# A two-layer mixture-of-experts kernel: x put in x1's column order by GpSimd ahead of time, and one exponential moved between two copies on ScalarE

## The chip, the cores and the metric

The kernel runs on one NeuronCore of a Trainium2 chip. The metric is the device time in microseconds, lower is better. TensorE (PE) multiplies matrices out of SBUF into PSUM, VectorE (DVE) and ScalarE (ACT) work on SBUF and PSUM, GpSimd (POOL) works on SBUF, and SyncE (SP) does nothing here but start transfers. Each engine runs its own list of instructions in order; they meet through semaphores.

## What is computed

The input x has 128 samples of 32 channels by 512 columns. Two layers follow one another, each adding to x:

```python
def cond0(x, embedding, ...):            # attention over 8 kernels, from the sample's embedding
    att = softmax(gelu(gelu(embedding @ W0 + b0) @ W1 + b1) @ W2 + b2)
    agg_w = einsum('bk,koi->boi', att, weight[..., 0])
    return einsum('boi,bih->boh', agg_w, x) + (att @ bias_k)[:, :, None]
def ffn0(y, W_up, gate_w, expert_bias, lora_A, lora_B):     # 4 experts of rank 8, top 1
    one_hot = argmax_one_hot(y @ gate_w.T + expert_bias)
    z = einsum('nh,erh->ner', y, lora_A)
    return y @ W_up.T + einsum('neh,ne->nh', einsum('ner,ehr->neh', z, lora_B), one_hot)
def cond1(x, c, weight, c_weight, bias):                    # 9-tap convolution in 4 groups
    out = conv1d(x, weight, pad=4, groups=4)
    return out + (c @ c_weight.T)[:, :, None] + bias[None, :, None]
def ffn1(c, W_base, b_base, W_gate, A, B):                  # 8 experts of rank 16, top 2
    route_w = top2_softmax_weights(c @ W_gate.T)
    h = einsum('bnd,erd->bner', c, A) * route_w[..., None]
    return c @ W_base.T + b_base + einsum('bner,eor->bno', h, B)
x = x + ffn0(cond0(x, cond_128, ...), ...)                  # called x1 below
out = x + ffn1(cond1(x, cond_128, ...), ...)
```

## The kernel before, in words

The 4096 rows (sample and channel) are cut into 32 tiles of 128 rows, that is 4 samples each. Matrix products run on float32 values split in two: a rounded high part (`y_hi`, `xq_hi`, `c_hi`) that ScalarE copies, and a low part (`y_lo`, `xq_lo`, `c_lo`), the difference, that GpSimd or VectorE computes; a product is then high by high, high by low and low by high.

Every engine has one function `body(i, par)`, called for i from 0 to 33. `iterate` (L241) writes out the calls 0 to 3 and 28 to 33 and makes a loop on the chip of 4 to 27, two to a turn. In `body(i)` three tiles are in work: tile i in layer 0, tile i-1 in layer 1's convolution and product, tile i-2 in the end of layer 1. `once(t)` is true where tile t exists, `after(engine, semaphore, count)` is a wait that is left out for counts of zero. `par` is i modulo 2: `xt`, the tile of x, has two buffers.

For tile t the work goes so. `mix` (L914) multiplies `xt` by the sample's weights; VectorE adds the bias into `y32`; `y_hi` on ScalarE and `y_lo` on GpSimd (L430) follow. TensorE then runs `up_half` for columns 256 to 511 with the gate (L854, L859, j = 1), and later for columns 0 to 255; `lora_delta` (L901) adds the expert's part. `x1_sum` (L674) adds x to that, in two halves, and writes `x1s`: x1 in another order of columns, p = (m j r) read as j, r, m, and shifted by one between the halves. SyncE and ScalarE copy `x1s` to `xq` with eight transfers of 32.5 KB (`move_x`, L277), five on SyncE's queue and three on ScalarE's; behind its five SyncE starts the load of tile t+2 into the same `xt` buffer (`load_x`, L284), then the store of an output. From `xq` come `xq_hi` (L507) and `xq_lo` (L415), each in two parts of 16 channels (gp = 0 and 1); GpSimd then computes `x1b` = x1 plus a bias in x's own order (L422), and `prod` (L369) for a tile further on.

TensorE's `body(i)` is, in order: `up_half` j = 1 of tile i; `conv(i-1, 0)`, with the transposition `turn_hw` in it; `conv(i-1, 1)`; `up_half` j = 0 of tile i, with the transposition `turn_z` in it; `lora_delta(i)`; the experts' product of tile i-2 (L987); `mix(i+1)`; the base product of tile i-1 (L1004 and L1009), whose first half writes over a PSUM bank that VectorE's `out_sum` (L708) has to have read. Each `conv(t, gp)` has four products of `xq_hi` and then two of `xq_lo`, for which it waits.

VectorE's order around the two places: `turn_c` of part 0, `z_low`, `turn_c` of part 1, `x1_sum(i)`, `out_sum` j = 0 of tile i-2, the two halves of `c_lo`, `out_sum` j = 1, `y_sum(i+1)`. In the gate of layer 1 the largest two logits (`m81`, L723) go to ScalarE for an exponential (`e2`, L501), and come back to VectorE for the route and `hw` (L740), which TensorE transposes in `turn_hw`. On ScalarE the exponential stands first in `body(i)`, then the two parts of `xq_hi`.

Of the kernel before, what the change touches and what calls it, by code (L numbers as in the profile page):

```python
# [5 lines left out]
ALU = mybir.AluOpType  # L6
# [6 lines left out]
P = 128  # L13
B = 128
C = 32
H = 512
SPT = P // C
NT = B // SPT
NQ = 4
# [12 lines left out]
GP = 2  # L32
# [12 lines left out]
def adaln_ffn(nc, x, cond, fside, W0, b0, W1, b1, W2, b2, wmix, bias_k, w_up, gate_w,  # L45
# [6 lines left out]
    with ExitStack() as ctx:  # L52
# [6 lines left out]
        def bank(name, banks=1):  # L59
# [57 lines left out]
        prod, gsum = sb("prod", [P, C, KATT]), sb("gsum", [P, C])  # L117
        mix_w = sb("mix_w", [P, SPT, C])
        y32, y_hi, y_lo = sb("y32", [P, KC, P]), sb("y_hi", [P, KC, P], F32R), sb("y_lo", [P, KC, P], F32R)
        gl0, m80, ix0 = sb("gl0", [P, 8]), sb("m80", [P, 8]), sb("ix0", [P, 8], U32)  # L120
# [45 lines left out]
                                                           sem("zt_done"), sem("zT_ready"))  # L166
        upgate_done, basegate_done = sem("upgate_done"), sem("basegate_done")
        lb_done, x1_done, x1b_done = sem("lb_done"), sem("x1_done"), sem("x1b_done")
        xqhi_done, xqlo_done, ct_done = sem("xqhi_done"), sem("xqlo_done"), sem("ct_done")
# [179 lines left out]
        def _(pool):  # L349
# [21 lines left out]


            pool.wait_ge(in_small0, 64)
            for n in range(3):
# [29 lines left out]
            pool.wait_ge(in_gate, 16)  # L404
            order_rows(g1_p, g1_raw, g1p_ready)
            pool.wait_ge(in_b1, 16)
            pool.tensor_copy(b1m_t[:], b1m_raw[:].rearrange("m e q r -> m q e r")).then_inc(b1_copied, 1)

            def body(i, par):
                if once(i - 1):  # L410

                    for gp in range(GP):
                        pool.wait_ge(xqhi_done, 2 * i - 1 + gp)
                        pool.wait_ge(xq_in[gp], i * XQ)
                        pool.tensor_tensor(xq_lo[:, gp], xq[:, gp], xq_hi[:, gp], ALU.subtract)\  # L415
                            .then_inc(xqlo_done, 1)
                    if isinstance(i, int) and i == 1:
                        pool.wait_ge(in_rows, 32)
                    pool.wait_ge(x1_done, 2 * i)
                    after(pool, out_done, (i - 2) * 2)  # L420
                    for j in range(2):
                        pool.tensor_tensor(columns_of(x1b[:, 1 - par])[:, j], shifted(j), columns_of(bbase_s[:])[:, j],  # L422
                                           ALU.add).then_inc(x1b_done, 1)
                if once(i + 3):
                    make_prod(i + 3)
                if once(i + 1):

# [7 lines left out]
        def _(act):  # L435
# [16 lines left out]
            def high_part(n):  # L452
# [6 lines left out]
                else:  # L459
                    act.activation(fills[n][4], fill_bank(n), ACT.Copy).then_inc(fill_hi, 1)  # L460

            def z_high(t):
# [33 lines left out]

            def body(i, par):
                if once(i - 2):

                    act.wait_ge(m81_ready, i - 1)  # L500
                    act.activation(e2[:], m81[:, 0:1], ACT.Exp, bias=m81[:, 1:2], scale=-1.0).then_inc(e2_ready, 1)  # L501
                if once(i - 1):

                    for gp in range(GP):
                        act.wait_ge(xq_in[gp], i * XQ)
                        after(act, conv_done, 2 * i - 3 + gp)
                        act.activation(xq_hi[:, gp], xq[:, gp], ACT.Copy).then_inc(xqhi_done, 1)  # L507
                if once(i - 2):
# [33 lines left out]
        def _(dve):  # L542
# [122 lines left out]
            def x1_sum(t, par):  # L665
# [4 lines left out]
                after(dve, xq_in[1], t * XQ)  # L670
                after(dve, x1b_done, 2 * t)
                for j in range(2):
                    dve.wait_ge(lb_done, 2 * t + j + 1)
                    dve.tensor_tensor(shifted(j), ps_up[:, j, 0:HALF].rearrange("p (r m) -> p r m", r=NQ),  # L674
                                      columns_of(xt[:, par])[:, j], ALU.add).then_inc(x1_done, 1)

# [361 lines left out]
```

## Time and profile before

| | |
|---|---|
| median of 3 runs | 380.35 us (377.62 to 380.48) |
| the profiled execution, its own time | 379.92 us |
| its span | 378.1 us, so 1.8 us lie outside the span |
| TensorE busy | 356.5 us, 94% of the span |
| VectorE, GpSimd, ScalarE busy | 284.5, 179.4, 135.5 us |

The span runs from the first to the last instruction. A matmul's end is modelled, and matmuls overlap, so that TensorE's pace is read from the distances between their ends. Times in the views are microseconds from the span's start; a name's digits are left out there (`y32` is y, `c32` is c, `e2` is e).

### The profile page before, as it was taken

To read this page: it belongs to the slowest core of one execution; us is meant where nothing else is said; L and a number is where in the kernel's file an instruction comes from. 1 tells how busy PE (TensorE), PEld (TensorE's weight loads), DVE (VectorE), ACT (ScalarE), POOL (GpSimd) and SP (SyncE) were. 2 spreads that over 40 slices of the span, in tenths; PEclk is the share of its full clock that TensorE was granted. 3 is DMA by queue.
4 is the path that set the end of the run, shared out by engine and by line. 5 is a ranking of instruction groups with operands and counts; after the bars stand their busy time and mean duration, and the time that the engine had idled before them with its cause. 6 is when DMAs were issued, how large, how long until landed. Compare 5 with 4: busy or idle time off the path is not lost.

```text
span 378.1 us, 8986 instructions
## 1 busy us (share of the span) xinstructions
PE 356.5 (94%) x2589; PEld 343.6 (91%) x2589; DVE 284.5 (75%) x966; ACT 135.5 (36%) x409; POOL 179.4 (47%) x223
## 2 busy tenths in 40 slices
PE   2877999999999999999999999999999999999975
PEld 1666999999999999999999999999999999999964
DVE  1675768787887887777788788777877878877653
ACT  2634243333333434433333343443333333343321
POOL 5364455544445455554444545555444454444430
PEclk9998699999999999999999999999999999999999
DMA  7622245343323323333332333333333233234221
GB/s 163 187 85 30 93 123 149 86 85 76 62 59 78 76 72 81 84 84 84 84 59 59 74 77 73 77 84 84 84 84 78 42 74 78 72 77 86 56 58 56
DMA packets 49983, 30.92 MB, mean 82 GB/s; under 512 B 39684, under 2 KB 40116, under 8 KB 49968
## 3 DMA queue, kind: packets, MB, share of 16 engines
q1 hardware_dynamic: 35744, 26.60, 28.2%
q10 hardware_dynamic: 13984, 3.73, 6.6%
q0 software_dynamic: 240, 0.41, 0.4%
q8 instruction: 7, 0.11, 0.1%
q14 instruction: 8, 0.07, 0.1%
HBM read 13.79 MB, written 8.40 MB: 59 GB/s over the span
## 4 chain that ended last, share of the span: by engine, by line
PE 86%; DVE 2%; POOL 1%; ACT 1%; DMA 1%; issue 1%; ACTq 1%; DVEq 0%; POOLq 0%
PE ps_base L1004 21%; PE ps_up L854 17%; PE ps_base L1009 10%; PE ps_up L859 8%; PE ps_mix L914 7%; PE ps_conv L876 6%; PE ps_mix L876 6%; PE ps_base L987 6%; PE ps_up L901 2%; PE ps_turn L893 1%; DMA xq<-x1s 1%; PE ps_turn L885 1%; ACTq L277 1%; POOL base_p L388 1%; PE ps_base L814 1%
## 5 line engine op out<-in xcount | busy, mean ns | idle before, releaser
L430 POOL TENSOR_TENSOR y_lo<-y,y_hi 128x512 fp32r<-128x512 f32 x31 | 40.1, 1295 | 141.0 <-ACT y_hi L478 141.0
L1004 PE MATMUL ps_base<-base_hi,c_hi 128*128 128x392 f32 (+1 forms) x256 | 78.6, 323 | 2.5 <-ACT c_hi L526 1.3
L1004 PE MATMUL ps_base<-base_lo,c_hi 128*128 128x392 f32 (+1 forms) x256 | 75.2, 311 | 0.0
L854 PE MATMUL ps_up<-up_hi,y_hi 128*128 128x292 f32 (+1 forms) x256 | 72.2, 304 | 1.2 <-ACT y_hi L478 1.2
L854 PE MATMUL ps_up<-up_lo,y_hi 128*128 128x292 f32 (+1 forms) x256 | 69.5, 293 | 0.0
L581 DVE TENSOR_TENSOR mix_w<-gsum,quad 128x64 f32<-128x64 f32 x64 | 39.2, 616 | 33.2 <-PE ps_base L1009 32.1
L415 POOL TENSOR_TENSOR xq_lo<-xq,xq_hi 128x260 fp32r<-128x260 f32 x64 | 46.6, 745 | 34.5 <-ACT xq_hi L507 24.8
L422 POOL TENSOR_TENSOR x1b<-x1s,bbase_s 128x256 f32<-128x256 f32 x64 | 57.0, 923 | 0.0
L1004 PEld LDWEIGHTS ps_base<-base_hi,c_hi 128*128 128x128 f32 x256 | 48.2, 188 | 8.2 <-issue 4.8
L854 PEld LDWEIGHTS ps_up<-up_hi,y_hi 128*128 128x128 f32 x256 | 49.2, 192 | 1.4 <-ACT y_hi L478 1.3
L478 ACT ACTIVATE y_hi<-y 128x512 fp32r<-128x512 f32 x32 | 20.2, 632 | 82.2 <-DVE y L591 78.9
L854 PEld LDWEIGHTS ps_up<-up_lo,y_hi 128*128 128x128 f32 x256 | 49.2, 192 | 0.0
L1009 PE MATMUL ps_base<-base_hi,c_lo 128*128 128x392 f32 (+1 forms) x256 | 48.4, 311 | 0.0
L1004 PEld LDWEIGHTS ps_base<-base_lo,c_hi 128*128 128x128 f32 x256 | 48.2, 188 | 0.0
L859 PE MATMUL ps_up<-up_hi,y_lo 128*128 128x292 f32 (+1 forms) x256 | 43.7, 293 | 0.0
L1009 PEld LDWEIGHTS ps_base<-base_hi,c_lo 128*128 128x128 f32 x256 | 40.4, 188 | 0.0
L674 DVE TENSOR_TENSOR x1s<-ps_up,xt 128x256 f32<-128x256 f32 x64 | 38.0, 636 | 2.2 <-PE ps_up L901 1.0
L859 PEld LDWEIGHTS ps_up<-up_hi,y_lo 128*128 128x128 f32 x256 | 37.0, 191 | 0.4 <-POOL y_lo L430 0.4
L914 PE MATMUL ps_mix<-mix_w,xt 128*128 128x128 f32 x256 | 33.8, 275 | 0.1
L507 ACT ACTIVATE xq_hi<-xq 128x260 fp32r<-128x260 f32 x64 | 26.5, 415 | 15.7 <-DMA xq<-x1s 15.5
L473 ACT ACTIVATE c<-ps_conv,biasT 128x64 f32<-128x64 f32 x128 | 29.7, 315 | 6.3 <-PE ps_conv L876 3.1
L914 PEld LDWEIGHTS ps_mix<-mix_w,xt 128*128 128x128 f32 x256 | 31.3, 191 | 0.3 <-issue 0.3
(164 smaller groups left out, 639.5 us busy)
## 6 DMA issues: line engine op xcount, KB each, us to landing
xt<-in_x SPq DMA_DIRECT2D x32, 256.0 KB, 2.8
out_x<-ot SPq DMA_DIRECT2D x32, 256.0 KB, 2.8
xq<-x1s SPq DMA_DIRECT2D x160, 32.5 KB, 2.2
xq<-x1s ACTq DMA_DIRECT2D x96, 32.5 KB, 2.2
rows<-agg_rows SPq DMA_DIRECT2D x2, 597.0 KB, 3.9
wbase_raw<-in_L_ffn_W_base SPq DMA_DIRECT2D x2, 512.0 KB, 4.3
rows<-agg_rows SPq DMA_DIRECT2D x1, 598.0 KB, 4.0
wup_raw<-in_L_ffn_W_up ACTq DMA_DIRECT2D x2, 256.0 KB, 4.6
```

The costliest lines, as they stand in the source:

```text
L415: pool.tensor_tensor(xq_lo[:, gp], xq[:, gp], xq_hi[:, gp], ALU.subtract)\
L422: pool.tensor_tensor(columns_of(x1b[:, 1 - par])[:, j], shifted(j), columns_of(bbase_s[:])[:, j], ALU.add).then_inc(x1b_done, 1)
L430: pool.tensor_tensor(y_lo[:], y32[:], y_hi[:], ALU.subtract).then_inc(ylo_done, 1)
L473: act.activation(c32[:, 0, cols], ps_of[0][:, 0, cols], ACT.Identity, bias=biasT[:, 0, bass.ds(t * SPT + b, 1)]).then_inc(c32_done, 1)
L581: dve.tensor_tensor(mix_w[:, b2], gsum[:].unsqueeze(1).to_broadcast([P, SPT // 2, C]), quad[:, b2].unsqueeze(2).to_broadcast([P, SPT // 2, ...
L674: dve.tensor_tensor(shifted(j), ps_up[:, j, 0:HALF].rearrange("p (r m) -> p r m", r=NQ), columns_of(xt[:, par])[:, j], ALU.add).then_inc(x ...
L854: pe.matmul(into, y_hi[:, k], w[:, k, cols], start=(k == 0 and w is up_hi), stop=False, skip_group_check=True)
L859: mm = pe.matmul(into, y_lo[:, k], up_hi[:, k, cols], start=False, stop=(k == KC - 1), skip_group_check=True)
L876: mm = pe.matmul(ps_of[gp][:, 0, 0:HALF], w[:, gp, part], rhs[:, gp, :, part:part + NB], start=(n == 0 and part == 0), stop=(n == 2 and pa ...
L914: mm = pe.matmul(ps_mix[:, 0, k * P:(k + 1) * P], xt[:, par, k * P:(k + 1) * P], mix_w[:].rearrange("p b o -> p (b o)"), start=True, stop= ...
L1004: pe.matmul(ps_base[:, j, 0:width], c_hi[:, q], w[:, q, j, 0:width], start=(q == 0 and w is base_hi), stop=False, skip_group_check=True)
L1009: mm = pe.matmul(ps_base[:, j, 0:width], c_lo[:, q], base_hi[:, q, j, 0:width], start=False, stop=(q == NQ - 1), skip_group_check=True)
```

## The change

There is a new buffer `xtp` with two halves, one for each `xt` buffer. GpSimd's new `order_x(t, par)` copies tile t of `xt` into it in x1's column order, and `x1_sum` reads `xtp` where it read `xt` through `columns_of`; for that it waits on `xtp_done`. `order_x(0, 0)` stands in GpSimd's preparation. In GpSimd's `body(i)`, `order_x(i + 1, 1 - par)` stands behind `prod` and ahead of `y_lo`. The wait for the transfer that it reads (tile i+1 in `xt`, semaphore `x_in`) stands at the head of `body(i)`, ahead of both parts of `xq_lo`; only in `body(0)` it stands at the copy itself. On ScalarE the copy of `xq_hi` is now a function `x_high`, called for part 0 ahead of the exponential and for part 1 behind it.

```diff
--- before.py
+++ after.py
@@ -116,6 +116,7 @@
         xt = sb("xt", [P, 2, H])
         prod, gsum = sb("prod", [P, C, KATT]), sb("gsum", [P, C])
         mix_w = sb("mix_w", [P, SPT, C])
+        xtp = sb("xtp", [P, 2, H])
         y32, y_hi, y_lo = sb("y32", [P, KC, P]), sb("y_hi", [P, KC, P], F32R), sb("y_lo", [P, KC, P], F32R)
         gl0, m80, ix0 = sb("gl0", [P, 8]), sb("m80", [P, 8]), sb("ix0", [P, 8], U32)
         zm = sb("zm", [P, 3, Z0])
@@ -165,6 +166,7 @@
         up_done, gate0_step, z_ready, zt_done, zT_ready = (sem("up_done"), sem("gate0_step"), sem("z_ready"),
                                                            sem("zt_done"), sem("zT_ready"))
         upgate_done, basegate_done = sem("upgate_done"), sem("basegate_done")
+        xtp_done = sem("xtp_done")
         lb_done, x1_done, x1b_done = sem("lb_done"), sem("x1_done"), sem("x1b_done")
         xqhi_done, xqlo_done, ct_done = sem("xqhi_done"), sem("xqlo_done"), sem("ct_done")
         conv_done, c32_done, chi_done, clo_done = sem("conv_done"), sem("c32_done"), sem("chi_done"), sem("clo_done")
@@ -370,6 +372,11 @@
                                    ALU.mult).then_inc(prod_done, 1)
 
 
+            def order_x(t, par):
+
+                pool.tensor_copy(xtp[:, par].rearrange("p (j r m) -> p j r m", j=2, r=NQ), columns_of(xt[:, par]))\
+                    .then_inc(xtp_done, 1)
+
             pool.wait_ge(in_small0, 64)
             for n in range(3):
                 cp = pool.tensor_copy(lb_rep[:, :, n], lb_raw[:].rearrange("m e q r -> m q e r"))
@@ -403,12 +410,16 @@
             order_rows(a1_p, a1_raw, a1p_ready)
             pool.wait_ge(in_gate, 16)
             order_rows(g1_p, g1_raw, g1p_ready)
+            pool.wait_ge(x_in[0], 16)
+            order_x(0, 0)
             pool.wait_ge(in_b1, 16)
             pool.tensor_copy(b1m_t[:], b1m_raw[:].rearrange("m e q r -> m q e r")).then_inc(b1_copied, 1)
 
             def body(i, par):
                 if once(i - 1):
 
+                    if once(i + 1):
+                        pool.wait_ge(x_in[1 - par], (i + par) * 8 + 16)
                     for gp in range(GP):
                         pool.wait_ge(xqhi_done, 2 * i - 1 + gp)
                         pool.wait_ge(xq_in[gp], i * XQ)
@@ -424,6 +435,10 @@
                 if once(i + 3):
                     make_prod(i + 3)
                 if once(i + 1):
+                    if not once(i - 1):
+                        pool.wait_ge(x_in[1 - par], 16)
+                    order_x(i + 1, 1 - par)
+                if once(i + 1):
 
                     pool.wait_ge(y32_done, i + 2)
                     pool.wait_ge(yhi_done, i + 2)
@@ -459,6 +474,12 @@
                 else:
                     act.activation(fills[n][4], fill_bank(n), ACT.Copy).then_inc(fill_hi, 1)
 
+            def x_high(i, gp):
+
+                act.wait_ge(xq_in[gp], i * XQ)
+                after(act, conv_done, 2 * i - 3 + gp)
+                act.activation(xq_hi[:, gp], xq[:, gp], ACT.Copy).then_inc(xqhi_done, 1)
+
             def z_high(t):
 
                 act.wait_ge(zt_done, t + 1)
@@ -495,16 +516,14 @@
             act.activation(conv_columns(conv_hi), conv_turns(), ACT.Copy).then_inc(convhi_ready, 1)
 
             def body(i, par):
+                if once(i - 1):
+                    x_high(i, 0)
                 if once(i - 2):
 
                     act.wait_ge(m81_ready, i - 1)
                     act.activation(e2[:], m81[:, 0:1], ACT.Exp, bias=m81[:, 1:2], scale=-1.0).then_inc(e2_ready, 1)
                 if once(i - 1):
-
-                    for gp in range(GP):
-                        act.wait_ge(xq_in[gp], i * XQ)
-                        after(act, conv_done, 2 * i - 3 + gp)
-                        act.activation(xq_hi[:, gp], xq[:, gp], ACT.Copy).then_inc(xqhi_done, 1)
+                    x_high(i, 1)
                 if once(i - 2):
 
                     act.wait_ge(ht_done, i - 1)
@@ -669,10 +688,12 @@
                 after(dve, xq_in[0], t * XQ)
                 after(dve, xq_in[1], t * XQ)
                 after(dve, x1b_done, 2 * t)
+                dve.wait_ge(xtp_done, t + 1)
                 for j in range(2):
                     dve.wait_ge(lb_done, 2 * t + j + 1)
                     dve.tensor_tensor(shifted(j), ps_up[:, j, 0:HALF].rearrange("p (r m) -> p r m", r=NQ),
-                                      columns_of(xt[:, par])[:, j], ALU.add).then_inc(x1_done, 1)
+                                      xtp[:, par, j * HALF:(j + 1) * HALF].rearrange("p (r m) -> p r m", r=NQ),
+                                      ALU.add).then_inc(x1_done, 1)
 
             def z_low(t):
 
```

The loop on the chip, GpSimd, one turn's first half before; each row is an instruction with what it waits for (ISA and REGISTER_ALU rows are waits and address arithmetic):

```order
L414 REGISTER_ALU [waits xqhi_done]
L415 TENSOR_TENSOR xq_lo<-xq,xq_hi 128x260 [waits xq_in0]
L415 TENSOR_TENSOR xq_lo<-xq,xq_hi 128x260 [waits xq_in1,xqhi_done]
L235 ISA [waits x1_done]
L422 TENSOR_TENSOR x1b<-x1s,bbase_s 128x4x64 [waits out_done]
L422 TENSOR_TENSOR x1b<-x1s,bbase_s 128x4x64
L235 ISA
L369 ISA [waits gsum_done]
L369 TENSOR_TENSOR prod<-wmix_t,att_b 128x256
L428 REGISTER_ALU
L430 TENSOR_TENSOR y_lo<-y,y_hi 128x512 [waits yhi_done,y32_done]
```

The same place now, as far as the copy:

```order
L424 ISA [waits x_in1]
L425 REGISTER_ALU [waits xqhi_done]
L426 TENSOR_TENSOR xq_lo<-xq,xq_hi 128x260 [waits xq_in0]
L426 TENSOR_TENSOR xq_lo<-xq,xq_hi 128x260 [waits xq_in1,xqhi_done]
L237 ISA [waits x1_done]
L433 TENSOR_TENSOR x1b<-x1s,bbase_s 128x4x64 [waits out_done]
L433 TENSOR_TENSOR x1b<-x1s,bbase_s 128x4x64
L237 ISA
L371 ISA [waits gsum_done]
L371 TENSOR_TENSOR prod<-wmix_t,att_b 128x256
L377 COPY xtp<-xt 128x512
```

The wait for x's transfer (`x_in`) is the first thing in the turn, and a copy of 512 columns stands between `prod` and `y_lo`.

ScalarE, the same turn before, from the exponential on:

```order
L501 ACTIVATE e<-m 128x1 [waits m81_ready]
L505 REGISTER_ALU
L235 ISA [waits xq_in0]
L507 ACTIVATE xq_hi<-xq 128x260 [waits conv_done]
L235 REGISTER_ALU [waits xq_in1]
L507 ACTIVATE xq_hi<-xq 128x260 [waits conv_done]
L511 ACTIVATE hT_hi<-ps_turn 128x128 [waits ht_done]
```

and now:

```order
L237 ISA [waits xq_in0]
L481 ACTIVATE xq_hi<-xq 128x260 [waits conv_done]
L523 REGISTER_ALU
L524 ACTIVATE e<-m 128x1 [waits m81_ready]
L237 REGISTER_ALU [waits xq_in1]
L481 ACTIVATE xq_hi<-xq 128x260 [waits conv_done]
L530 ACTIVATE hT_hi<-ps_turn 128x128 [waits ht_done]
```

The exponential has moved behind part 0 of `xq_hi` and no longer stands ahead of it.

## Rows read from the trace of the kernel before

**Rows 1.** Busy time by stretch: stretch, length, engines busy, TensorE's granted clock, DMA share, GB/s.

```profile
38.00:44.00 6.00, 5.58 (x25) 5.25 (x25) 4.47 (x14) 1.81 (x7) 3.84 (x5) 0.50 0.36 146
200.00:320.00 120.00, 119.85 (x896) 117.17 (x895) 98.08 (x332) 43.17 (x138) 58.15 (x68) 1.00 0.34 73
364.00:378.00 14.00, 8.54 (x51) 7.06 (x50) 5.28 (x20) 3.16 (x11) 3.19 (x4) 1.00 0.18 61
```

**Rows 2.** Timeline, one body's tail: start, length, engine, instruction, count, idle before it.

```profile
201.81 1.21 DVE L674 TENSOR_TENSOR x1s<-ps_up,xt 128x256 f32<-128x256 f32 x2
202.40 1.05 PE L914 MATMUL ps_mix<-mix_w,xt 128*128 128x128 f32 x8
202.91 0.44 DVE L708 TENSOR_TENSOR ot<-ps_base,x1b 128x256 f32<-128x256 f32 x1
203.25 0.77 DVE L786 TENSOR_TENSOR c_lo<-ps_ct,c_hi 128x256 fp32r<-128x256 f32 x2
203.48 0.19 PEld L1004 LDWEIGHTS ps_base<-base_hi,c_hi 128*128 128x128 f32 x1 [0.22 <-issue]
```

**Rows 3.** Timeline of SyncE's queue, the same body.

```profile
203.05 3.45 SPq L277 DMA_DIRECT2D xq<-x1s  x5
206.72 0.41 SPq L284 DMA_DIRECT2D xt<-in_x  x1
```

**Rows 4.** The 24 loads of x issued from 85 to 335 us (L284).

```profile
L284 SPq DMA_DIRECT2D xt<-in_x x24: 341/376/590, 91.9 to 332.7; - x24
DMA to landing us min/median/max: 2.4/2.8/3.2
```

**Rows 5.** Timeline of GpSimd, the body that follows.

```profile
205.80 1.29 POOL L430 TENSOR_TENSOR y_lo<-y,y_hi 128x512 fp32r<-128x512 f32 x1 [4.39 <-ACT y_hi L478]
208.06 1.44 POOL L415 TENSOR_TENSOR xq_lo<-xq,xq_hi 128x260 fp32r<-128x260 f32 x2 [0.97 <-DMA xq<-x1s]
209.47 1.81 POOL L422 TENSOR_TENSOR x1b<-x1s,bbase_s 128x256 f32<-128x256 f32 x2
211.25 0.73 POOL L369 TENSOR_TENSOR prod<-wmix_t,att_b 128x256 f32<-128x256 f32 x1
```

**Rows 6.** Timeline of ScalarE and TensorE around the convolution, same body.

```profile
207.30 0.30 ACT L501 ACTIVATE e<-m 128x1 f32<-128x1 f32 x1 [1.64 <-DVE m L723]
207.50 0.41 ACT L507 ACTIVATE xq_hi<-xq 128x260 fp32r<-128x260 f32 x1
...
209.29 0.49 PE L876 MATMUL ps_conv<-xq_lo,conv_hi 128*128 128x256 f32 x2
...
212.29 1.18 DVE L674 TENSOR_TENSOR x1s<-ps_up,xt 128x256 f32<-128x256 f32 x2
```

**Rows 7.** Timeline near the end, where TensorE waits for `xq_lo`.

```profile
364.75 0.74 POOL L415 TENSOR_TENSOR xq_lo<-xq,xq_hi 128x260 fp32r<-128x260 f32 x1 [7.65 <-ACT xq_hi L507]
...
365.54 0.51 PE L876 MATMUL ps_conv<-xq_lo,conv_hi 128*128 128x256 f32 x2
```

**Rows 8.** Groups by shape: count, busy us, mean ns of one, idle before.

```profile
L674 DVE TENSOR_TENSOR x1s<-ps_up,xt 128x256 f32<-128x256 f32 x64 | 38.0, 636 | 2.2 <-PE ps_up L901 1.0
L708 DVE TENSOR_TENSOR ot<-ps_base,x1b 128x256 f32<-128x256 f32 x64 | 26.8, 420 | 0.7 <-PE ps_base L987 0.7
L565 DVE TENSOR_TENSOR base_lo<-ps_base,base_hi 128x512 fp32r<-128x512 f32 x3 | 2.1, 692 | 4.0 <-ACT base_hi L460 4.0
L565 DVE TENSOR_TENSOR b_lo<-ps_base,b_hi 128x512 fp32r<-128x512 f32 x1 | 1.1, 1112 | 0.3 <-ACT base_hi L460 0.3
L388 POOL COPY base_p<-wbase_raw 128x256 f32<-128x256 f32 x8 | 4.8, 642 | 0.0
```

**Rows 9.** Timeline, tiles 1 and 30, the ends of the stretch that repeats.

```profile
45.19 1.16 DVE L674 TENSOR_TENSOR x1s<-ps_up,xt 128x256 f32<-128x256 f32 x2 [0.41 <-PE ps_up L901]
...
348.23 1.19 DVE L674 TENSOR_TENSOR x1s<-ps_up,xt 128x256 f32<-128x256 f32 x2
```

## The prediction

> **What bounds the kernel now.** First the busy times by stretch: between 200 and 320 us TensorE is busy 119.85 of 120 us at a granted clock of 1.00, the full 2.4 GHz, while VectorE and GpSimd have 98.1 and 58.2 [rows 1]. So TensorE's list of work sets the pace, and only what holds TensorE up, or stops holding it up, moves the time. Then the two ends of the stretch that repeats: x1_sum of tile 1 starts at 45.19, of tile 30 at 348.23 [rows 9], so one body takes (348.23 - 45.19) / 29 = 10.45 us. Then the timeline of one body, for holes in TensorE's work. There is one: mix ends at 202.40 + 1.05 = 203.45, and the weight load of the base product starts at 203.48 after 0.22 us of idle time [rows 2]. The view gives "issue" as the reason, but that product also waits until out_sum j = 0 has read the bank, and out_sum runs from 202.91 to 203.35; it stands on VectorE behind the two x1_sums, which take 1.21 us. VectorE is thus on the path there, for about 0.22 us a body. Everywhere else the feeders come in time: xq_lo starts on GpSimd at 208.06, its first part is done at about 208.80, and TensorE takes it at 209.29 [rows 5, 6]. That slack is 0.5 us, and it matters below.
>
> **x1_sum reads xtp.** One x1_sum of 256 columns takes 636 ns, out_sum of 256 columns, PSUM and SBUF inputs too, 420 [rows 8]. The difference in form is that columns_of(xt) takes every eighth column. A second pair says that such a step costs: the low part b_lo, written and read in steps of four columns, took 1112 ns for 512, base_lo in long runs 692 [rows 8]. I take the new x1_sum at out_sum's price; a pair of such instructions takes 0.77 us (c_lo, [rows 2]), against 1.21, so 0.44 us less. The bounds are 0.77 and 1.21, the second if the step is not the cause. On the path this is worth at most the hole: out_sum would end before mix does, and 0.22 us a body is gained.
>
> The Trainium skill, "VectorE: DVE Perf Modes", section "Mode 1× (REGULAR) — the baseline", says that this mode makes no assumption on strides and gives one result per cycle, and its section "The TRN2 errata" gives (N + 151) / 0.96 ns for an fp32 tensor_tensor, 424 ns for 256 columns. By that rule the strided form should have cost 424 ns already and the excess would have another cause and stay; out_sum's row agrees with the figure, x1_sum's and b_lo's do not.
>
> **The copy order_x on GpSimd.** 512 columns in steps of eight: the nearest row is the COPY in steps of eight with 642 ns for 256 [rows 8], so 1.28 us a body; the bounds are that and 1.81, the time of the pair x1b with steps on two operands [rows 5]. It stands behind prod, which ends at 211.98, and ahead of y_lo, before which GpSimd is idle for 4.39 us in one body [rows 5]. That idle time is its cover, so it costs nothing; should GpSimd be late for y_lo by a microsecond, TensorE's y_lo products would wait for it. The copy for tile 0 stands in the preparation where GpSimd later idles too.
>
> **The exponential.** Before, ScalarE waits 1.64 us for the maximum from VectorE, does the exponential at 207.30, and part 0 of xq_hi at 207.50 [rows 6]. Now part 0 goes into that idle time. Its only reader before TensorE is xq_lo, which could start when y_lo ends, at 207.09, and not at 208.06 [rows 5]. TensorE needs neither before 209, so the gain is zero by itself; the worst is a body in which part 0 comes late and puts the exponential back by its 0.41 us, which the same slack of half a microsecond covers. I take zero.
>
> **The wait for x's transfer at the head of GpSimd's body.** This is the term that decides. In body i GpSimd now waits for tile i+1 in xt ahead of both parts of xq_lo. Who starts that transfer? SyncE, in its body i-1, behind the five copies of x1s of tile i-1, and xq_lo in GpSimd's body i works on just these copies. Before the change xq_lo depended on the copies; now it depends on the sixth transfer of the same queue as well. In the trace x1_sum ends at 203.02, the first copy starts at 203.05 and the load at 206.72 [rows 2, 3]; it lands 2.8 us after its issue, 2.4 to 3.2 over 24 loads [rows 4], here between 209.1 and 209.9 and by the median at 209.5. But xq_lo starts at 208.06 before the change [rows 5]. Behind the waiting GpSimd are queued both parts of xq_lo, x1b, prod and the copy; TensorE waits for xq_lo part 0 in conv(i-1, 0), and with it all that stands behind in its list, up to the x1_sum that starts the next load. So it is a closed loop that no slack can hide, and the new length of a body is its sum:
>
> - the pair of x1_sums, 0.77;
> - end of x1_sum to the start of the load, 206.72 - 203.02 = 3.70 [rows 2, 3];
> - the load's landing, 2.8 [rows 4];
> - GpSimd's start after it: xq_lo started 0.15 after xq_hi's end (207.50 + 0.41 to 208.06, [rows 5, 6]), and I take 0.2, as a wait and an address instruction now stand in between;
> - start of xq_lo part 0 to TensorE's first product on it, where TensorE does wait: 365.54 - 364.75 = 0.79 [rows 7];
> - that product to the next x1_sum: 212.29 - 209.29 = 3.00 [rows 6]. This piece is a chain through TensorE, ScalarE and VectorE, all behind the convolution, so it moves as a whole.
>
> The sum is 0.77 + 3.70 + 2.8 + 0.2 + 0.79 + 3.00 = 11.26 us, 0.81 more than 10.45. It holds 29 times between tiles 1 and 30: 23.5 us. (Tile 0 to 1 has room: TensorE runs there at half clock from 38 to 44 us [rows 1].) Behind tile 30 no load is left to wait for, and there the old gains come: 0.22 for the hole and 0.44 for the last x1_sum, 0.7 us. The profiled execution was 379.92, and 0.1% under the median of 380.35, so both serve: 379.92 + 23.5 - 0.7 = 402.7, **403 us**.
>
> The gain of the hole is not to be added: TensorE reaches the convolution earlier by it and waits there longer. The faster x1_sum is in the sum, since x1_sum itself is a part of the loop. x1b has to be ready for the next x1_sum: it ends 3.22 us after xq_lo's start [rows 5], x1_sum comes 0.79 + 3.00 = 3.79 after it, so 0.57 us are left.
>
> **The rivals.**
> First, the forecast's mechanism, with x1_sum unchanged at 636 ns: 0.44 more for 29 bodies and the last, 13 us, so 416. For it speaks the page's rule above, against it the two pairs of rows; chance 0.08.
>
> Second, the other side: the wait costs nothing, because x is there when GpSimd asks. It would have to land by about 208.3, the slack of 0.5 us behind xq_lo's present start used up; that is 1.6 us from the start of its issue, where the shortest of 24 took 2.4. Or the count that GpSimd waits for would be that of the tile before; but (i + par) * 8 + 16 is the count that mix waits for as tile i+1's. Then only the hole remains: 31 bodies by 0.22 and the last x1_sum, 7.3 us, so 373. The point where it flips is the landing at 1.6 us. Chance 0.06.
>
> Third, the same loop, but shorter: landing 2.4 and GpSimd's start 0.15, thus 10.81 a body, 13 us less, 390. A single load can be that quick, the mean of all hardly; chance 0.04.
>
> Fourth, TensorE's clock falls because of the new pauses of about a microsecond a body. It was at 0.50, that is 1.2 GHz, from 38 to 44 us after a start with holes, but at 1.00 in the last 14 us with TensorE busy 8.54 of 14 [rows 1], which is far emptier than the 10.2 of 11.3 to come. If the piece of 3.00 us ran at the low level in one body of four, it would add up to 3 us in each of those seven, 21 us: 424. Chance 0.03.
>
> **How the numbers follow.** The forecast as worked out has 0.79. Its own spread: landing 2.8 with a mean off by 0.15 gives 4 us either way, GpSimd's start between 0.15 and 0.3 gives -1.5 to +3, SyncE's 3.70 with 0.1 gives 3; so 396 to 411. To leave out no more than 2 in 10, the range goes up to the first rival: **395 to 417**. Left out are the second to fourth rivals. A change within 1% cannot be told from none for this kernel. Faster by over 1%: 0.06, the second rival. Within 1%: 0.02, for something between it and the forecast. Slower by over 1%: 0.92.
>
> **What would show it.** In the profile after: in GpSimd's timeline xq_lo part 0 starts right behind the landing of the load of x, not behind xq_hi, and the chain that ended last runs through the transfer xt<-in_x, GpSimd's xq_lo and VectorE's x1_sum, with a body of 11.3 us; TensorE is idle for about 1 us a body ahead of L876's products on xq_lo, and its busy share falls to about 90%; xq_hi part 0 ends a microsecond or more ahead of its xq_lo; the new COPY takes about 1.3 us with GpSimd idle behind it; x1_sum takes 0.42 us; and TensorE's clock stays at 1.00. The forecast is wrong if TensorE does not wait at that product, or if the load lands much sooner after its issue than it did.

## Result and the profile after

The changed kernel takes **407.23 us** (median of 4 runs, 405.49 to 408.67), the kernel before, run on the same chip, 380.17 (4 runs, 377.62 to 380.48). The ratio is 1.0726 with the interval 1.066 to 1.0791: slower by 7.3%. The forecast was 403, with a range of 395 to 417.

The profiled execution took 405.49, with a span of 403.7 us against 378.1 before. The page gives the same work for more time: TensorE has 355.6 us of it, 88% of the span. The shares of the engines in the chain of work that ended last read

```profile
PE 25%; SPq 18%; DMA 18%; issue 11%; POOL 8%; DVE 8%; ACTq 2%; ACT 2%; DVEq 1%; POOLq 1%
```

In the kernel before PE alone had 86% of that chain. Here SyncE's queue and the transfers hold 36% of it, and the lines named first behind this row are the copies of `x1s` (L279, 18%) and the load of x (`xt<-in_x`, 15%).

The busy times by stretch (stretch, length, busy time of TensorE, its weight loads, VectorE, ScalarE, GpSimd, granted clock, DMA share, GB/s) answer to [rows 1]:

```profile
38.00:44.00 6.00, 4.82 (x38) 4.43 (x37) 4.64 (x19) 2.10 (x8) 4.68 (x6) 1.00 0.34 133
44.00:56.00 12.00, 10.56 (x65) 10.06 (x64) 5.65 (x25) 3.68 (x12) 6.44 (x8) 0.86 0.38 98
200.00:320.00 120.00, 111.10 (x828) 108.62 (x828) 85.91 (x302) 41.60 (x128) 66.47 (x75) 1.00 0.30 67
```

TensorE is now idle for 8.9 of 120 us where it was idle for 0.15, and its clock is still at 1.00. The view of the waits (engine, operation, line and what it waited for: us in total, times, the longest) says for what:

```profile
POOL y_lo L445 <- ACT y_hi L499: 81.9, 31, 4.2
POOL xq_lo L426 <- DMA xt<-in_x: 75.3, 30, 3.2
PEld ps_conv L897 <- POOL xq_lo L426: 32.2, 30, 2.0
PE ps_conv L897 <- POOL xq_lo L426: 25.2, 30, 1.7
```

GpSimd waits 30 times, once a body, for the load of x ahead of `xq_lo`, and TensorE waits 30 times for that `xq_lo`. The timeline of one body shows the order in time (start, length, engine, instruction, count, idle time before it and what ended it); the rows of before are [rows 2, 3, 5, 6]:

```profile
225.15 0.76 DVE L694 TENSOR_TENSOR x1s<-ps_up,xtp 128x256 f32<-128x256 f32 x2
225.93 3.46 SPq L279 DMA_DIRECT2D xq<-x1s  x5
...
229.09 0.42 ACT L481 ACTIVATE xq_hi<-xq 128x260 fp32r<-128x260 f32 x1 [0.47 <-DMA xq<-x1s]
...
229.72 0.34 SPq L286 DMA_DIRECT2D xt<-in_x  x1
...
232.71 1.44 POOL L426 TENSOR_TENSOR xq_lo<-xq,xq_hi 128x260 fp32r<-128x260 f32 x2 [2.66 <-DMA xt<-in_x]
...
233.50 0.50 PE L897 MATMUL ps_conv<-xq_lo,conv_hi 128*128 128x256 f32 x2 [0.92 <-POOL xq_lo L426]
...
236.52 0.76 DVE L694 TENSOR_TENSOR x1s<-ps_up,xtp 128x256 f32<-128x256 f32 x2
236.57 1.15 POOL L377 COPY xtp<-xt 128x512 f32<-128x512 f32 x1
```

Read it downwards: part 0 of `xq_hi`, which `xq_lo` needs, is done at 229.51, and GpSimd starts `xq_lo` only at 232.71, when the load has landed that was issued at 229.72. TensorE sits idle for 0.92 us until 233.50, and 3.02 us behind that stands the next `x1_sum`, whose copies go ahead of the next load. One turn is 236.52 - 225.15 = 11.37 us.

Two groups by shape answer to [rows 8] (count, busy us, mean ns of one, idle before):

```profile
L694 DVE TENSOR_TENSOR x1s<-ps_up,xtp 128x256 f32<-128x256 f32 x64 | 24.2, 420 | 2.6 <-PE ps_up L922 1.4
L377 POOL COPY xtp<-xt 128x512 f32<-128x512 f32 x32 | 37.5, 1172 | 0.0
```

**Where the 25.6 us of span went.** `x1_sum` of tile 1 starts at 43.13 and that of tile 30 at 373.50, so a body takes (373.50 - 43.13) / 29 = 11.39 us, 0.94 more than 10.45 [rows 9]: 29 of them are 27.3 us. Tile 1 comes 2.1 us earlier than in [rows 9], the body from tile 30 to 31 is 0.3 shorter, and what follows tile 31 is 0.6 longer: 27.3 - 2.1 - 0.3 + 0.6 = 25.5, the 25.6 to within the rounding.

### The profile page after: what moved, and what is told of

Its sections match the earlier page's. It is cut to its first block, busy times and chain, and to the rows that moved or that the text cites. A ratio compares the mean times of both kernels' runs of the same rounds, so it can differ in the third digit from the quotient of the medians.

```text
span 403.7 us, 9066 instructions
## 1 busy us (share of the span) xinstructions
PE 355.6 (88%) x2589; PEld 342.6 (85%) x2589; DVE 273.9 (68%) x966; ACT 138.3 (34%) x409; POOL 214.5 (53%) x255
## 3 DMA queue, kind: packets, MB, share of 16 engines
q10 hardware_dynamic: 13984, 3.73, 6.2%
## 4 chain that ended last, share of the span: by engine, by line
PE 25%; SPq 18%; DMA 18%; issue 11%; POOL 8%; DVE 8%; ACTq 2%; ACT 2%; DVEq 1%; POOLq 1%
SPq L279 18%; DMA xt<-in_x 15%; POOL xq_lo L426 6%; PE ps_up L875 5%; PE ps_mix L897 5%; DVE x1s L694 4%; PE ps_conv L897 4%; DMA xq<-x1s 3%; PE ps_up L880 3%; DVE ps_ct L721 3%; ACTq L279 2%; PE ps_base L1025 2%; POOL x1b L433 1%; PE ps_up L922 1%; PE ps_base L1030 1%
## 5 line engine op out<-in xcount | busy, mean ns | idle before, releaser
L600 DVE TENSOR_TENSOR mix_w<-gsum,quad 128x64 f32<-128x64 f32 x64 | 37.9, 596 | 34.5 <-PE ps_base L1030 33.3
L897 PE MATMUL ps_conv<-xq_lo,conv_hi 128*128 128x256 f32 x64 | 16.1, 333 | 25.2 <-POOL xq_lo L426 25.2
L377 POOL COPY xtp<-xt 128x512 f32<-128x512 f32 x32 | 37.5, 1172 | 0.0
L897 PEld LDWEIGHTS ps_conv<-xq_lo,conv_hi 128*128 128x128 f32 x64 | 9.5, 188 | 32.2 <-POOL xq_lo L426 32.2
```

What stands on the lines that cost most here:

```text
L377: pool.tensor_copy(xtp[:, par].rearrange("p (j r m) -> p j r m", j=2, r=NQ), columns_of(xt[:, par]))\
L600: dve.tensor_tensor(mix_w[:, b2], gsum[:].unsqueeze(1).to_broadcast([P, SPT // 2, C]), quad[:, b2].unsqueeze(2).to_broadcast([P, SPT // 2, ...
L897: mm = pe.matmul(ps_of[gp][:, 0, 0:HALF], w[:, gp, part], rhs[:, gp, :, part:part + NB], start=(n == 0 and part == 0), stop=(n == 2 and pa ...
```

## Experiments

Two theories stood against the one on record once the result was known. **The wait** (mine): the loss is the closed loop through the load of x, and nothing else of the change costs anything. **The copy**: GpSimd has 37.5 us more work, and is late with what follows. **The exponential**: part 0 of `xq_hi`, or what stands behind it, comes late. A fourth question was whether the loop's length is really set by where the load stands in SyncE's queue. Each ratio below is to the kernel before on the same chip, which took 378.9 to 379.3 us there.

**The wait moved.** The changed kernel, with the wait for x taken from the head of GpSimd's body and put behind `x1b`, ahead of `make_prod`, where by the forecast's rows the load has landed. The same transfers, copies and instructions are left.

```diff
                 if once(i - 1):
-                    if once(i + 1):
-                        pool.wait_ge(x_in[1 - par], (i + par) * 8 + 16)
                     for gp in range(GP):
...
+                if once(i - 1) and once(i + 1):
+                    pool.wait_ge(x_in[1 - par], (i + par) * 8 + 16)
                 if once(i + 3):
                     make_prod(i + 3)
```

> The changed kernel with one line moved: GpSimd waits for x's transfer behind x1b, just ahead of prod and the copy, and no longer at the head of its body. Loop theory (the wait closes a loop x1_sum, five copies, load of x, xq_lo, convolution, x1_sum of 11.37 us): the loop is gone, TensorE's list sets the pace again, and what is left are the gains, 31 holes of 0.22 us and 0.44 at the end, so about 373 us (ratio 0.98), a body of 10.2 us, no idle time of TensorE at xq_lo. Rival, the copy's load: the 1.17 us that GpSimd has more to do in each body make xq_lo late; then moving the wait gives back little, and the time stays above 395.

Measured: 372.55 us (6 runs, 371.66 to 374.2), ratio to before 0.984 (0.9804 to 0.9876). Moving one wait past four instructions turns a loss of 27.1 us against the kernel before into a gain of 6.3. A body is 10.23 us ((349.85 - 43.03) / 30, tiles 1 to 31). GpSimd's timeline, with SyncE's load of the same body at 231.54, shows what the wait had kept back:

```profile
226.19 1.20 POOL L377 COPY xtp<-xt 128x512 f32<-128x512 f32 x1
230.59 1.28 POOL L445 TENSOR_TENSOR y_lo<-y,y_hi 128x512 fp32r<-128x512 f32 x1 [3.20 <-ACT y_hi L499]
231.83 0.75 POOL L424 TENSOR_TENSOR xq_lo<-xq,xq_hi 128x260 fp32r<-128x260 f32 x1
233.38 0.74 POOL L424 TENSOR_TENSOR xq_lo<-xq,xq_hi 128x260 fp32r<-128x260 f32 x1 [0.80 <-ACT xq_hi L481]
234.07 1.81 POOL L431 TENSOR_TENSOR x1b<-x1s,bbase_s 128x256 f32<-128x256 f32 x2
235.79 0.79 POOL L371 TENSOR_TENSOR prod<-wmix_t,att_b 128x256 f32<-128x256 f32 x1
```

`xq_lo` starts right behind `y_lo`, only 0.29 us after the load has been issued; `prod` starts 4.25 us after it, well past the landing, so the moved wait holds nobody. TensorE's busy time from 80 to 320 us is full:

```profile
80.00:320.00 240.00, 240.00 (x1836) 239.08 (x1835) 197.68 (x684) 92.01 (x284) 148.89 (x166) 1.00 0.35 77
```

**The wait alone.** The kernel before, with nothing of the change but the wait.

```diff
                 if once(i - 1):
+                    if once(i + 1):
+                        pool.wait_ge(x_in[1 - par], (i + par) * 8 + 16)
                     for gp in range(GP):
```

> The kernel before with nothing but the new wait at the head of GpSimd's body; no copy, no xtp, the exponential where it was. Loop theory: the same loop with the old pair of x1_sums, 11.37 + 0.44 = 11.81 us a body, 1.36 more than 10.45, 29 times: 39 us, so about 419 us (ratio 1.10), slower than the changed kernel. Rival, the copy's load: 380 us, as there is no copy.

Measured: 421.97 us (4 runs, 420.88 to 424.33), ratio 1.1138 (1.1081 to 1.1195). A body is 11.91 us ((391.60 - 46.23) / 29), 0.52 more than in the changed kernel; the two `x1_sum`s, slower by 0.43 here, are part of the loop and make most of that. Its waits:

```profile
POOL xq_lo L417 <- DMA xt<-in_x: 80.4, 30, 3.9
PEld ps_conv L878 <- POOL xq_lo L417: 40.6, 30, 3.4
```

The wait alone costs 43 us, more than the whole change with its 27; the rest of the change gives 16 of them back.

**The exponential's new place alone.** The kernel before, with part 0 of `xq_hi` ahead of the exponential and part 1 behind it.

```diff
             def body(i, par):
+                if once(i - 1):
+                    x_high(i, 0)
                 if once(i - 2):
...
                 if once(i - 1):
-                    for gp in range(GP):
-                        ...
+                    x_high(i, 1)
```

> The kernel before with nothing but the exponential between the two parts of xq_hi. Loop theory with all slack as read: within 1% of 380 us, xq_hi part 0 a microsecond earlier, xq_lo part 0 right behind y_lo, and TensorE where it was. Rival, lost to contention: xq_lo right behind y_lo keeps VectorE's second mix_w back (the first one already takes 1.08 us where it falls beside y_lo, the second 0.23), hw comes 0.5 us later and TensorE waits for it up to 0.3 us a body: about 385 to 390 us.

Measured: 381.86 us (12 runs, 379.2 to 382.9), ratio 1.0066 (1.0039 to 1.0093). It is within 1%, but the interval leaves out 1: some 2.5 us are lost. A body is 10.48 us ((359.39 - 45.05) / 30), against 10.45, and the difference is one body at the start (tile 1 to 2, 10.98 against 10.14); those that repeat take 10.46 in both. What follows tile 31's `x1_sum` takes 20.8 us (380.2 - 359.39), against 19.5 before. So the larger part of the loss is in the last body that has both instructions; the timeline there:

```profile
365.33 0.42 ACT L466 ACTIVATE xq_hi<-xq 128x260 fp32r<-128x260 f32 x1 [5.34 <-DMA xq<-x1s]
365.66 0.28 ACT L509 ACTIVATE e<-m 128x1 f32<-128x1 f32 x1
...
366.95 0.14 PEld L889 LDWEIGHTS ps_turn<-ident,hw 128*128 128x128 f32 x1 [2.38 <-DVE hw L744]
```

The maximum `m` had been there since 363.57 (its `MAX8` starts at 363.40 and takes 0.17). The exponential had to wait behind `xq_hi`, for copies of tile 31's `x1s`, and TensorE waits 2.38 us for `hw`, which follows the exponential.

**The old order in the last body.** The same kernel, but with the exponential first in body 32.

```diff
             def body(i, par):
-                if once(i - 1):
+                exp_first = isinstance(i, int) and i == NT
+                if once(i - 1) and not exp_first:
                     x_high(i, 0)
                 if once(i - 2):
...
                 if once(i - 1):
+                    if exp_first:
+                        x_high(i, 0)
                     x_high(i, 1)
```

> The kernel before with the exponential between the two parts of xq_hi in every body except body 32, where it stands ahead of both as before. Theory: the 0.66% that the exponential's move cost alone come from body 32 only, where no tile is left to hide the transfers of xq and TensorE waited 2.2 us for hw behind part 0 of xq_hi; so this one is within 0.3% of the kernel before, and that wait is back at some 0.3 us. Rival, contention in every body (xq_lo right behind y_lo keeps mix_w back): the 0.66% stay.

Measured: 380.1 us (12 runs, 378.3 to 381.34), ratio 1.0017 (0.9987 to 1.0046). The wait of TensorE there is 0.35 us:

```profile
363.51 0.29 ACT L510 ACTIVATE e<-m 128x1 f32<-128x1 f32 x1 [3.65 <-DVE m L730]
364.42 0.35 DVE L747 SCALAR_TENSOR_TENSOR hw<-ps_base,erec,route 128x128 f32<-128x128 f32 x1
364.82 0.14 PEld L892 LDWEIGHTS ps_turn<-ident,hw 128*128 128x128 f32 x1 [0.35 <-DVE hw L747]
```

What follows tile 31 takes 19.3 us again (378.5 - 359.25). So 1.3 to 1.6 us of the loss are this one wait in one body out of 32, shown by a run at either side. Whether anything of the loss is left without it these runs can't tell: the interval here goes up to 0.5%.

**Neither the wait nor the exponential's place.** The kernel with the wait moved, and the exponential where it was before: the copy and the new `x1_sum` are all that is left of the change.

```diff
             def body(i, par):
-                if once(i - 1):
-                    x_high(i, 0)
                 if once(i - 2):
...
                 if once(i - 1):
-                    x_high(i, 1)
+                    for gp in range(GP):
+                        ...
```

> The kernel with xtp, x1_sum reading it, the wait ahead of prod as in the run with the wait moved, and the exponential ahead of both parts of xq_hi as before the change. Loop theory: 373 us, the same as with the exponential moved, since that move is worth nothing. Rival for the exponential: if its move costs (xq_lo right behind y_lo keeping mix_w back), this one is faster than the run with the wait moved by 3 to 9 us; if it helps, slower.

Measured: 371.27 us (6 runs, 369.72 to 373.39), ratio 0.9801 (0.9761 to 0.9842), a body of 10.22 us ((350.76 - 44.25) / 30). With the next one, 371.16, it is the fastest, 2.0% under the kernel before. From the kernel with the wait moved it differs by 1.3 us, which the two intervals do not tell apart; but in the profiles that difference stands where the exponential's should, behind tile 31: 20.8 us there (370.6 - 349.85) and 19.1 here (369.9 - 350.76).

**The copy done twice.** That kernel with `order_x` made twice as long: a first copy goes into a buffer that nobody reads.

```diff
             def order_x(t, par):
+                pool.tensor_copy(xtq[:, par].rearrange("p (j r m) -> p j r m", j=2, r=NQ), columns_of(xt[:, par]))
                 pool.tensor_copy(xtp[:, par].rearrange("p (j r m) -> p j r m", j=2, r=NQ), columns_of(xt[:, par]))\
```

> The run with the copy alone, with GpSimd's copy done twice, the first time into a buffer that nobody reads. It prices the copy's cover. Theory: GpSimd is idle for about 3 us ahead of y_lo (93.9 us over 31 bodies), another 1.17 us fits in, and the time stays within 1% of 371 us. Rival, the cover ends early: every microsecond that is not covered counts 30 times, so 1.17 us of it would give up to 406 us.

Measured: 371.16 us (4 runs, 370.39 to 371.4), ratio 0.9791 (0.9734 to 0.9847): 36.7 us more of GpSimd's copies (74.9 against 38.2) cost nothing. Nearly all of them came out of the idle time before `y_lo`, 93.9 us in the kernel with one copy and here

```profile
POOL y_lo L446 <- ACT y_hi L500: 59.5, 31, 2.8
```

So the copy was hidden, twice over. The theory of the copy falls.

**The load earlier or later in SyncE's queue.** Three kernels, each the changed one with only the place of `load_x(i + 2, par)` in SyncE's body moved: behind four of the five copies, behind three of them, and behind the store of `ot`. In the sum on record every issue ahead of the load is a part of the loop, so each should count 29 times.

```diff
                         for b in range(SPT // 2 + gp):
+                            if gp == 1 and b == SPT // 2 and (not isinstance(i, int) or i + 2 < NT):
+                                load_x(i + 2, par)
                             move_x(sp, gp, b)
-                    if not isinstance(i, int) or i + 2 < NT:
-                        load_x(i + 2, par)
```

> The changed kernel with SyncE's load of x issued behind four of its five copies, not behind all five. Everything else stays, the wait at the head of GpSimd's body too. Loop theory: the loop is shorter by one issue on SyncE, 3.46 / 5 = 0.69 us, so 11.39 - 0.69 = 10.70 us a body, 29 times: 20 us less than 407.2, about 387 us (ratio 1.02). Rival (GpSimd's wait costs through what it keeps from running behind it, not through when x lands): no more than 1% from 407.

Behind three of the copies (the same edit with `b == 1`):

> The same, with the load behind three of the five copies. Loop theory: the loop would be 11.39 - 1.38 = 10.01 us, shorter than TensorE's own 10.22 us a body as measured with the wait moved; so TensorE sets the pace again and the time is that of the run with the wait moved, 372 to 374 us, though the wait still stands at the head. A straight line from the run before would give 367. Rival: about 407 as above.

Behind the store:

```diff
                     sp.dma_start(out_rows[bass.ds((i - 2) * P, P), :], ot[:, par]).then_inc(stored[par], 16)
+                if once(i) and (not isinstance(i, int) or i + 2 < NT):
+                    load_x(i + 2, par)
```

> The changed kernel with the load of x behind the store of the output, the next transfer on SyncE's queue. Loop theory: the loop is longer by that issue, 230.34 - 229.72 = 0.62 us, so 12.01 us a body and 18 us more: about 425 us (ratio 1.12). Rival: 407 us.

Measured, with the body as the mean from tile 1 to tile 30:

| load stands behind | time, us | runs | ratio to before | body, us |
|---|---|---|---|---|
| 3 copies | 373.78 (372.56 to 374.66) | 4 | 0.9856 (0.9797 to 0.9915) | 10.29 |
| 4 copies | 383.03 (381.55 to 383.83) | 8 | 1.0092 (1.0051 to 1.0132) | 10.63 |
| 5 copies (the change) | 407.23 (405.49 to 408.67) | 4 | 1.0726 (1.066 to 1.0791) | 11.39 |
| 5 copies and the store | 429.67 (427.92 to 432.11) | 4 | 1.1342 (1.1261 to 1.1424) | 12.13 |

Nothing but the place of one issue was edited, and the time follows it. The means in the table hold the first bodies, which differ from kernel to kernel. From tile 4 to tile 30 a body takes 10.62, 11.35 and 11.82 us for four copies, five, and five and the store: (349.98 - 73.76) / 26, (373.50 - 78.44) / 26 and (398.34 - 91.05) / 26. In these bodies the load is issued 3.11, 3.75 and 4.35 us behind the end of the `x1_sum`s in the mean, so one issue is worth 0.64 and 0.60 us; the rest of the steps of 0.73 and 0.47 comes mostly from `xq_lo`'s start, 2.92, 3.04 and 2.90 us behind the load's issue. From four copies to three the whole mean falls by only 0.34, to near the 10.22 of TensorE's own work. In the kernel with three copies GpSimd still waits for the load in all 30 bodies, but TensorE doesn't wait for GpSimd any more; of its products on `xq_lo` the only wait left is the second row:

```profile
POOL xq_lo L425 <- DMA xt<-in_x: 32.8, 30, 1.5
...
PEld ps_mix L896 <- POOL xq_lo L425: 0.8, 3, 0.3
```

In the kernel with the load behind the store it is the reverse, and the idle times grow:

```profile
POOL xq_lo L425 <- DMA xt<-in_x: 94.2, 30, 4.5
...
PEld ps_conv L896 <- POOL xq_lo L425: 51.4, 30, 3.1
```

Two of the expectations missed by some microseconds. With four copies 387 was expected. The body came out 0.07 shorter than the 10.70 expected, 2 us over 29, and tile 1 started at 41.72, 1.4 earlier than in the changed kernel. In one body of it the wait ahead of `xq_lo` ends with a copy of `x1s`, not with the load; this is so 22 times of 30. SyncE's timeline:

```profile
226.26 0.42 SPq L286 DMA_DIRECT2D xt<-in_x  x1
226.72 0.55 SPq L279 DMA_DIRECT2D xq<-x1s  x1
```

and in GpSimd's timeline of the same body

```profile
229.16 1.44 POOL L425 TENSOR_TENSOR xq_lo<-xq,xq_hi 128x260 fp32r<-128x260 f32 x2 [1.69 <-DMA xq<-x1s]
```

The release still stands 2.90 us behind the issue of the load, and the last copy was issued 0.46 behind it. By the code it is the load that released it: part 0 of `xq_lo` waits for no other transfers than the load and the copies that part 0 of `xq_hi` waits for too, and that one had started at 226.39. With the load behind the store 425 was expected and 429.67 came. There the miss is at the start: tiles 1 to 4 take 14.86 us each ((91.05 - 46.48) / 3), the other 26 bodies up to tile 30 11.82 ((398.34 - 91.05) / 26), and the clock is low in the first ones only:

```profile
46.00:62.00 16.00, 12.71 (x78) 12.31 (x78) 6.64 (x28) 4.32 (x14) 6.17 (x8) 0.81 0.30 73
62.00:77.00 15.00, 12.28 (x79) 12.05 (x79) 8.16 (x29) 3.66 (x12) 6.14 (x7) 0.86 0.38 94
77.00:91.00 14.00, 11.84 (x80) 11.60 (x79) 8.25 (x29) 3.39 (x12) 6.16 (x7) 0.88 0.26 58
91.00:103.00 12.00, 11.06 (x85) 10.82 (x84) 8.66 (x31) 4.02 (x14) 5.54 (x7) 1.00 0.28 67
```

Two things make the three bodies long. The piece from TensorE's product to the next `x1_sum` takes 5.20, 4.54 and 4.43 us in them and 3.02 later. And in the first two `xq_lo` starts 4.17 and 4.81 us behind the load's issue, not 2.90. There the edit puts the load behind one more transfer, the 0.6 MB of `rows` that SyncE issues in its bodies 0 to 2:

```profile
65.83 0.59 SPq L337 DMA_DIRECT2D rows<-agg_rows  x1
66.46 0.43 SPq L341 DMA_DIRECT2D out_x<-ot  x1
66.94 0.43 SPq L286 DMA_DIRECT2D xt<-in_x  x1
```

That `rows` made these two loads late isn't shown: in the kernel with the wait alone one load at the start was as late (4.74 us, issued at 74.15), with no `rows` ahead of it in that body.

## Why the prediction was right, and where it was off

**The bound and the hole.** Right. The hole of 0.22 us ahead of the base product is gone wherever the load doesn't bind: a body takes 10.22 and 10.23 us in the two kernels without the wait at the head, and TensorE is busy for 240.00 of 240 us. That is the 0.22 a body of the text to within 0.01. In the changed kernel the base product follows without idle time as well, but the gain is spent waiting at the convolution, as the prediction said.

**The wait closes a loop.** Right, and shown by four kinds of run: moved, alone, and with the load one issue earlier and one later. Term by term, from the timeline above (225.15 to 236.52):

| term | predicted | measured | mean of 29 bodies |
|---|---|---|---|
| pair of x1_sums | 0.77 | 0.76 | 0.76 |
| their end to the load's issue | 3.70 | 3.81 (229.72 - 225.91) | 3.73 |
| landing and GpSimd's start | 2.8 + 0.2 | 2.99 (232.71 - 229.72) | 3.04 |
| xq_lo to TensorE's product | 0.79 | 0.79 (233.50 - 232.71) | 0.79 |
| product to next x1_sum | 3.00 | 3.02 (236.52 - 233.50) | 3.07 |
| sum | 11.26 | 11.37 | 11.39 |

The mean is 0.13 above the sum on record, and that is 3.8 us. With tile 1 earlier by 2.1 and 1.0 missing at the end (below), the profiled execution comes out 2.7 over the 402.7 of the working, as it did (405.49); the median lies 1.7 above that one. The sum left out what single bodies do. The body from tile 1 to 2 took 13.06 us, at a granted clock of 0.86 (the second row of the windows above), 1.7 more than a usual one; 1.5 of that are in the last term, 4.55 us. And SyncE's issues are sometimes slow: in the body from tile 28's start at 350.46 to 362.60, which is 12.14 long, the five copies took 4.19 us and not 3.46:

```profile
351.25 4.19 SPq L279 DMA_DIRECT2D xq<-x1s  x5
355.48 0.59 SPq L286 DMA_DIRECT2D xt<-in_x  x1
```

In the kernel before the five copies of this tile, the first behind the loop on the chip, took 4.09 us too (from 328.59), and its body was no longer than the others (10.45): the delay fell into slack. In a closed loop it counts in full. What makes the issues of this body slow isn't known.

**x1_sum.** Right: 420 ns each, `out_sum`'s figure to the nanosecond. What changed in it is the step of eight in one operand, and the buffer that operand lies in, so the first rival, which left it at 636, is refuted by that row and by the time (416 wanted, 407 measured). The rule of the Trainium skill behind that rival, "VectorE: DVE Perf Modes", section "Mode 1× (REGULAR) — the baseline", that the baseline mode takes any stride at one result per cycle, does not hold for this operand; the figure of its section "The TRN2 errata", 424 ns, is met by the form without the step alone.

**The copy.** Hidden, as said; it took 1.17 us and not 1.28. Twice its length was hidden too, in the kernel without the wait at the head.

**The exponential.** This step failed, if with little weight. The text put the move at zero, and it cost 1.3 to 1.6 us, once. It gave as the worst 0.41 us a body, covered by the slack of half a microsecond. In the repeating bodies that held. In body 32 there is no such cover: ScalarE idles for over 5 us until the copies for `xq_hi` have landed, the maximum is there 2 us before that, and the exponential stands behind `xq_hi`. The profile after has the same; the exponential starts at 389.74, 2.3 us after the end of the maximum, and VectorE waits for it:

```profile
387.30 0.17 DVE L744 MAX8 m<-ps_base 128x8 f32<-128x8 f32 x1 [1.51 <-PE ps_base L1030]
...
390.05 0.15 DVE L750 TENSOR_SCALAR den<-e 128x1 f32<-128x1 f32 x1 [2.29 <-ACT e L524]
```

A gain of 0.7 us was foreseen for the end. The last body brought 0.3, and what follows tile 31 cost 0.6.

**The rivals.** The second (373) was what the kernel does once the wait stands elsewhere: 372.55. It did not apply because the load lands 2.8 us after its issue (2.5 to 3.3 over 24 loads), as in [rows 4], and not within 1.6. The third (390) fell with the same figure. Of the fourth, the clock, there is a trace: the one body at 0.86, in which the piece priced at 3 us more took 1.5 more (4.55 against 3.02). In the stretch that repeats the clock stayed at 1.00 with TensorE waiting for 0.84 us a body (25.2 / 30), and with some 1.3 a body behind the store too.

**What stays open.** The starts differ by up to 5 us between kernels (tile 1 at 41.72 to 46.48), and so does the clock from 38 to 44 us: 0.50 in the kernel before [rows 1], 1.00 in the changed one, 0.87 with the load behind the store. With the wait alone the clock was at 0.53 there, and at 0.50 with the old order in the last body, so the low start isn't the kernel before's alone. There is one profile of each, and it isn't settled how much of that is the kernel and how much the run. It bears on the result: tile 0 to 1 took 12.83 us before and 10.88 in the changed kernel, which is nearly all of the 2.1 us by which tile 1 came earlier.

**The spread.** 396 to 411 does not follow from its three terms; added up straight they give 394.5 to 413. The measured time lies within either.

## What to carry to other kernels

A wait at the head of an in-order queue is paid by everything behind it, so it belongs ahead of the first instruction that needs it. Before placing one, ask who starts the thing that is waited for, and behind what: if that stands behind work that this queue itself feeds, the wait closes a loop, and the loop's sum, not the slack, gives the time. An instruction that is moved is to be priced in the first and last bodies as well, where the work that covered it is missing.

## What the runs showed of the hardware that was not expected

- One operand read in steps of eight float32 columns costs VectorE half as much again: 636 ns for 256 columns [rows 8], 420 without the step.
- GpSimd's copy in steps of eight takes 1172 ns for 512 columns; its copy of `b1m_raw` into `b1m_t` in the kernel before, 512 columns too but in another order, takes 0.60 us.
- VectorE's `mix_w`, with both operands in SBUF, takes 0.23 us by itself and 0.58 or about 1 us when GpSimd is at work. In the kernel with the exponential's new place alone the timeline of GpSimd has

```profile
207.92 0.75 POOL L415 TENSOR_TENSOR xq_lo<-xq,xq_hi 128x260 fp32r<-128x260 f32 x1
```

  and that of VectorE the second half of `mix_w` beside it:

```profile
208.16 0.58 DVE L585 TENSOR_TENSOR mix_w<-gsum,quad 128x64 f32<-128x64 f32 x1
```

  It ends at 208.74, just behind the end of `xq_lo` at 208.67, as the first half (206.96 and 1.09 long) ends at 208.05 behind a `y_lo` that ends at 207.97. In the kernel before the second half (207.30) fell between two instructions of GpSimd and took 0.23. So `hw` starts 2.50 us behind the start of `mix_w` here, and 2.17 before. The 0.33 us were hidden.
- With the load behind the store, TensorE's clock was granted at 0.81 to 0.88 over the first three bodies, in which it waited for `xq_lo` for 2.6 us each, and at 1.00 in later ones, with 1.3 us each. In all three the pause came first: TensorE was idle from 53.79 to 56.68, from 69.82 to 72.54 and from 84.45 to 86.62, the clock was still at 1.00 from 54 to 56 and through the second and third, and over the 4 to 5 us that followed it was at 0.50, 0.64 and 0.56. So the low clock did not make these pauses; it made what came behind them longer. In the changed kernel the one fall, to 0.55 from 52.0 to 55.8, followed on 1.4 us of idle time between 48 and 52, where later bodies have 0.84.
